# Eight layer norms on one core: the mean's scaling folded into its subtraction, and the squares moved to ScalarE in all but one of them

## The reference

```python
def _ln_c(v, eps=1e-06):
    m = jnp.mean(v, axis=-1, keepdims=True)
    s = jnp.var(v, axis=-1, keepdims=True)
    return (v - m) / jnp.sqrt(s + eps)
...
    x = x + _L0_conv_ref(_ln_c(x), ...)
    t = _to_tokens(x)
    t = t + _L0_ffn_ref(_ln_t(t), ...)
...
    x = x + _L3_conv_ref(_ln_c(x), ...)
    t = _to_tokens(x)
    t = t + _L3_ffn_ref(_ln_t(t), ...)
```

## Time and profile before

| what | value |
|---|---|
| median of three runs | 1205.78 us (1204.79 to 1205.86) |
| the profiled execution's own time | 1202.41 us |
| its span | 1200.6 us |
| PE busy | 747.2 us (62%) |
| PEld busy | 435.2 us (36%) |
| DVE busy | 479.7 us (40%), 828 instructions |
| ACT busy | 454.9 us (38%), 1547 instructions |
| POOL busy | 226.0 us (19%) |

### The profile page before, as it was taken

The page is one execution under the profiler, slowest core; times in us unless marked ns, Lnnn a source line. Parts: engine busy times, 40 slices in busy tenths (PEclk is TensorE's granted clock), DMA queues, the critical chain, the costliest instruction groups (busy, mean ns, idle before and its releaser), DMA issues. The chain is left out here.

```text
span 1200.6 us, 11335 instructions
## 1 busy us (share of the span) xinstructions
PE 747.2 (62%) x4114; PEld 435.2 (36%) x4114; DVE 479.7 (40%) x828; ACT 454.9 (38%) x1547; POOL 226.0 (19%) x130
## 2 busy tenths in 40 slices
PE   4807777777767655545555555557995555548975
PEld 1302222232233323223333333335773333325753
DVE  5597999999855534500000000012020000018652
ACT  3446556565424422033333333332212333335531
POOL 2276666666600000020000000000000000002200
PEclk9956999999995575555555555555555555555995
DMA  2020000000000000100000000000000000000000
GB/s 61 1 53 1 0 1 0 1 0 1 0 5 1 1 20 9 58 1 1 1 1 1 1 0 1 1 1 1 1 1 1 1 1 1 1 1 1 1 20 10
DMA packets 9570, 7.68 MB, mean 6 GB/s; under 512 B 7154, under 2 KB 8066, under 8 KB 9224
## 3 DMA queue, kind: packets, MB, share of 16 engines
q1 hardware_dynamic: 9512, 6.93, 2.4%
HBM read 5.09 MB, written 0.26 MB: 4 GB/s over the span
## 5 line engine op out<-in xcount | busy, mean ns | idle before, releaser
L791 PE MATMUL L2p_z<-L2yx,L2v 64*32 64x2 f32 x2048 | 267.9, 199 | 242.1 <-ACT L2yx L801 236.3
L801 ACT ACTIVATE L2yx<-L2p_z 32x2 f32<-32x2 f32 x1024 | 165.2, 161 | 389.2 <-PE L2p_z L791 389.2
L791 PEld LDWEIGHTS L2p_z<-L2yx,L2v 64*32 64x32 f32 x2048 | 180.4, 135 | 340.0 <-ACT L2yx L801 316.0
L692 DVE COPY xn<-L2yx 32x512 f32<-32x512 f32 x2 | 0.8, 417 | 431.1 <-ACT L2yx L801 264.2
L573 POOL TENSOR_TENSOR hc<-hs,cb 128x1024 f32<-128x1024 f32 x64 | 150.9, 2358 | 81.6 <-DVE hs L560 81.6
L560 DVE TENSOR_TENSOR_SCAN hs<-d_a,p_bb 128x1024 f32<-128x1024 f32 x64 | 146.3, 2286 | 8.9 <-ACT d_a L539 0.7
L526 PE MATMUL p_y<-hc,ident 128*128 128x512 f32 x256 | 122.5, 602 | 3.4 <-POOL hc L573 3.0
L1498 POOL COPY xo<-xn 64x256 f32<-64x256 f32 (+1 forms) x6 | 3.9, 691 | 555.9 <-DVE xn L157 555.9
L539 ACT ACTIVATE d_a<-step,decay 128x1016 f32<-128x1016 f32 x64 | 73.1, 1142 | 86.9 <-DVE hs L560 86.4
L510 PE MATMUL p_bb<-b_parts,pick 96*128 96x512 bf16 x128 | 40.5, 399 | 81.9 <-DVE hs L560 49.2
L555 DVE TENSOR_TENSOR p_bb<-drive,p_bb 128x1024 f32<-128x1024 f32 x64 | 77.3, 1207 | 6.2 <-PE p_bb L510 6.2
(11 more groups left out here) (387 smaller groups left out, 854.5 us busy)
## 6 DMA issues: line engine op xcount, KB each, us to landing
y_seq<-in_pick SPq DMA_DIRECT2D x1, 768.0 KB
b_parts<-part SPq DMA_DIRECT2D x3, 256.0 KB, 3.6
c_parts<-part SPq DMA_DIRECT2D x3, 256.0 KB, 4.4
pos<-in_pos SPq DMA_DIRECT2D x1, 512.0 KB, 3.6
ao<-in_at_o SPq DMA_DIRECT2D x1, 512.0 KB, 4.4
L1w<-in_L_w SPq DMA_DIRECT2D x1, 297.0 KB
L3w<-in_L_w SPq DMA_DIRECT2D x1, 297.0 KB
x_tok<-in_x SPq DMA_DIRECT2D x2, 128.0 KB, 2.8
```

What stands on the lines that cost most here:

```text
L791: pe.matmul(p_z[0:C, t % 2, 0:NB], v[:, 0:C], yx[:, NB * t:NB * (t + 1)], start=True, stop=True).then_inc(s("preact"), 1)
L801: act.activation(yx[0:C, NB * (t + 1):NB * (t + 2)], p_z[0:C, t % 2, 0:NB], ACT.Sigmoid).then_inc(s("state"), 1)
```

## The change

In every norm, the instruction that scales the sums (L139) goes, and the subtraction becomes one `scalar_tensor_tensor`, (sum x -1/32) + tile, with the constant in the instruction. In the seven norms whose halves alternate, ACT now makes the squares (function `Square`), after the load of the root's table and ahead of the roots, on a new semaphore `ln_centred`; DVE waits for it with `ln_squared`. In the norm with `apart=True` DVE still makes the squares. `ln_stat` has a row less. All else is as it was; the lines that follow in the file are two further down.

```diff
--- before.py
+++ after.py
@@ -83,7 +83,7 @@
         xn = sb("xn", [R, T])
         xn_tok = sb("xn_tok", [128, T // 128, R])
         ln_sq = sb("ln_sq", [128, 2, 4 * R])
-        ln_stat = sb("ln_stat", [128, 2, 5, 4 * NB])
+        ln_stat = sb("ln_stat", [128, 2, 4, 4 * NB])
         ln_warm = sb("ln_warm", [128, 1])
 
         ln_uses = [0]
@@ -106,7 +106,7 @@
 
             def step(self, i, h):
 
-                return sig["ln_step"], 10 * self.k + (5 * h + i if self.apart else 2 * i + h) + 1
+                return sig["ln_step"], 4 * self.k + (2 * h + i if self.apart else 2 * i + h) + 1
 
             def turn(self, pe, h, j):
                 t = (4 * h + j) * 128
@@ -136,21 +136,20 @@
                     dve.tensor_reduce(ln_stat[:, h, 0], by_token(self.turned[h]), AX_X, ALU.add).then_inc(sig["ln_step"], 1)
                 for h in hs:
                     dve.wait_ge(*self.step(0, h))
-                    dve.tensor_scalar(ln_stat[:, h, 1], ln_stat[:, h, 0], 1.0 / C, None, ALU.mult).then_inc(sig["ln_step"], 1)
+                    dve.scalar_tensor_tensor(by_token(tok(h)), spread(ln_stat[:, h, 0]), -1.0 / C, by_token(self.turned[h]),
+                                             ALU.mult, ALU.add).then_inc(sig["ln_centred"], 1)
+                if self.apart:
+                    for h in hs:
+                        dve.wait_ge(*self.at("ln_centred", h))
+                        dve.tensor_tensor(ln_sq[:, h], tok(h), tok(h), ALU.mult).then_inc(sig["ln_squared"], 1)
                 for h in hs:
-                    dve.wait_ge(*self.step(1, h))
-                    dve.tensor_tensor(by_token(tok(h)), by_token(self.turned[h]), spread(ln_stat[:, h, 1]), ALU.subtract).then_inc(sig["ln_step"], 1)
-                for h in hs:
-                    dve.wait_ge(*self.step(2, h))
-                    dve.tensor_tensor(ln_sq[:, h], tok(h), tok(h), ALU.mult).then_inc(sig["ln_step"], 1)
-                for h in hs:
-                    dve.wait_ge(*self.step(3, h))
-                    dve.tensor_reduce(ln_stat[:, h, 2], by_token(ln_sq[:, h]), AX_X, ALU.add).then_inc(sig["ln_square"], 1)
+                    dve.wait_ge(*self.at("ln_squared", h))
+                    dve.tensor_reduce(ln_stat[:, h, 1], by_token(ln_sq[:, h]), AX_X, ALU.add).then_inc(sig["ln_square"], 1)
                 for h in hs:
                     dve.wait_ge(*self.at("ln_sd", h))
-                    dve.reciprocal(ln_stat[:, h, 4], ln_stat[:, h, 3]).then_inc(sig["ln_step"], 1)
-                    dve.wait_ge(*self.step(4, h))
-                    dve.tensor_tensor(by_token(tok(h)), by_token(tok(h)), spread(ln_stat[:, h, 4]), ALU.mult).then_inc(sig["ln_scaled"], 1)
+                    dve.reciprocal(ln_stat[:, h, 3], ln_stat[:, h, 2]).then_inc(sig["ln_step"], 1)
+                    dve.wait_ge(*self.step(1, h))
+                    dve.tensor_tensor(by_token(tok(h)), by_token(tok(h)), spread(ln_stat[:, h, 3]), ALU.mult).then_inc(sig["ln_scaled"], 1)
                 if self.apart:
                     for h in hs:
                         dve.wait_ge(*self.at("ln_back", h))
@@ -158,11 +157,14 @@
 
             def act_roots(self, act, h):
                 act.wait_ge(*self.at("ln_square", h))
-                act.activation(ln_stat[:, h, 3], ln_stat[:, h, 2], ACT.Sqrt, bias=self.eps[:, 0:1], scale=1.0 / C).then_inc(sig["ln_sd"], 1)
+                act.activation(ln_stat[:, h, 2], ln_stat[:, h, 1], ACT.Sqrt, bias=self.eps[:, 0:1], scale=1.0 / C).then_inc(sig["ln_sd"], 1)
 
             def act(self, act):
 
                 act.activation(ln_warm[:], self.eps[:], ACT.Sqrt)
+                for h in range(2):
+                    act.wait_ge(*self.at("ln_centred", h))
+                    act.activation(ln_sq[:, h], xn_tok[:, 4 * h:4 * h + 4].rearrange("p j r -> p (j r)"), ACT.Square).then_inc(sig["ln_squared"], 1)
                 for h in range(2):
                     self.act_roots(act, h)
                 for h in range(2):
```

## The result

| | before | change |
|---|---|---|
| median, first runs | 1205.82 us (1204.79 to 1205.87, 4 runs) | 1197.13 us (1196.91 to 1198.47, 4 runs) |
| mean over more executions | 1204.3 us (74, all later) | 1197.4 us (9) |
| the profiled execution's own time, span | 1202.41, 1200.6 us | 1196.91, 1195.0 us |
| DVE, ACT, PE busy | 479.7, 454.9, 747.2 us | 473.9, 459.6, 747.5 us |

The ratio is 0.9932, 95% interval 0.9915 to 0.9949. The forecast was 1201.7 us with a range of 1199.9 to 1204.4: the direction was right, the gain was 8.7 us instead of 4.1, and the time fell outside the range. The second line already takes 1.8 us off the riddle: the four executions of the kernel before in the first line lay high, and over many the two kernels are 6.9 us apart. 6.9 is still not 4.1.

What follows compares the result with a forecast made beforehand. No engine is busy throughout, so time is a sum of stages, with DVE the one to relieve in the norms. Savings 3.15 + 0.63 + 0.13 + 0.20 = 4.11 us gave 1205.78 - 4.1 = 1201.7 us, range 1199.9 to 1204.4.

Steps and rivals of the forecast that it cites:

- The price of the folded form: Every norm: the one-instruction subtraction costs +0.00 us over the old one, +0.06 at most, saving the scaling's 0.20.
- ACT's square: Norms with alternating halves: a square of 256 elements on ACT takes 0.42 us, helping save 0.43 a norm.
- the handoffs: Norms with squares on ACT: passing from DVE to ACT takes 0.04 us and back 0.03.
- the 0.48 and 0.15 from under the memset: L0_ffn and L2_ffn: extra savings because the scaling held by POOL's memset is gone; 0.63 us together.
- the weights being late next in the expert blocks: Expert blocks: PE's gate load also waits for transfers, so 0.13 us of 1.26 is saved and 1.13 lost.
- the 0.20 in L3_conv: L3_conv norm: half 0 is hidden beside the recurrence; half 1 gains only the scaling, 0.20 us.
- Rival 1: Expert blocks: weights landed earlier than SP's wait tells, saving 1.26 us instead of 0.13; 5.2 saved, 1200.5; chance 0.08.
- Rival 2: L0_ffn, L2_ffn: POOL's memset holds the new subtraction as it held the scaling; 3.1 us saved, 1202.7; chance 0.12.
- Rival 3: Squares on ACT: square or handoffs take 0.43 us more, so handing over gains nothing; 1.96 left, 1203.8; chance 0.12.
- I take the same 4.1 off the median: Whole kernel: the 4.11 us summed from the profile comes off the median, 1205.78 - 4.1 = 1201.7.
- rival 4: L1_conv: PE's clock rises later, 0.4 us per pass, up to 8 us (1209.7); chance 0.10, of which 0.06 slower.

Runs made afterwards that it cites:

- Experiments 3: Kernel before with only the scaling folded into the subtraction in all eight norms, DVE still making the squares; 1200.97 us, ratio 0.9971.
- experiment 4: Kernel before with only the squares moved to ACT in seven norms, the scaling staying its own instruction; 1200.18 us, ratio 0.996.
- experiment 6: The change, with PE waiting only for the gate's two transfers before the logits and for the expert weights later; 1197.22 us, ratio 0.9945.
- experiment 5: Kernel before with POOL's memset in the two recurrent blocks moved behind the norm's last multiplication; 1203.74 us, ratio 0.9997.
- 7: Kernel before with four extra, overwritten 64-row matmuls ahead of the L1_conv convolution; 1205.29 us, ratio 1.0003.
- experiment 13: The change with two extra, overwritten matmuls filling PE's pause in the window attention; 1198.49 us, ratio 0.9954.
- 11: Kernel before with two overwritten 128-row matmuls filling PE's 2.0 us pause in the window attention; 1202.97 us, ratio 0.9989.
- 14: The change with both a delay of about 1.95 us after the second recurrence and PE's attention pause filled by two matmuls; 1200.43 us, ratio 0.9967.
- 10: The change with three waited-for DVE memsets behind the second recurrence, a delay of 1.95 us; 1201.52 us, ratio 0.9974.
- 12: The change with four overwritten 128-row matmuls ahead of the L1_conv convolution to warm PE's clock; 1197.98 us, ratio 0.9946.
- 15: The change with the gate's transfers waited for apart, 128-row warming matmuls before the convolution and PE's attention pause filled; 1196.96 us, ratio 0.9937.
- 8: The change with four extra, overwritten 64-row matmuls ahead of the L1_conv convolution; 1197.9 us, ratio 0.9947.

## Why the prediction was wrong in size

**The mechanism and each term held.** The price of the folded form (0.42, like a `tensor_tensor`), ACT's square (0.416), the handoffs (0.03 to 0.04), the 0.48 and 0.15 from under the memset, the weights being late next in the expert blocks, the 0.20 in L3_conv: the table of norms has them all, with 0.22 instead of 0.13 in the expert blocks. Experiments 3 and 4 separate the two halves of the change and find each at its price.

**Rival 1** (weights landed earlier) is refuted by the grown gap ending with the transfer, and by experiment 6. **Rival 2** (the memset holds the new subtraction) is refuted by the row at 354.73, and its premise, that the memset held the scaling, confirmed by experiment 5. By the rule that the prediction cited from the Trainium skill ("SBUF — State Buffer", section "SBUF: two separate sides"), the subtraction with one input in PSUM runs freely; the trace agrees (0.74 for two beside the memset, 0.74 elsewhere). The scaling pair's 0.66 beside the memset against 0.29 behind it is the measured other side. **Rival 3** (handing over is worth nothing) is refuted by experiment 4. The rule of the Trainium skill that wants multiplications on VectorE ("ScalarE: Activation LUTs", section "Rules for kernel authors") gives speed as its reason; here ACT's square was as quick (0.416 us), and the overlap of the halves was the gain.

**The step that failed** is the one between the sum and the time: "I take the same 4.1 off the median". It treated the norms' 4.1 us as the whole difference, and the clock as a matter of one to four passes in L1_conv, as likely to help as to hurt (rival 4). The clock's crossing in the L3_conv attention, which moves with everything ahead of it, was put at nothing without a look, and so was the pause behind it. Three things stood in the place of this step.

1. *The base.* The 1205.78 was the median of three high executions; 74 later ones average 1204.3. That is 1.5 us that have nothing to do with the change, and no row could have told it.
2. *The rise in the window attention.* Four profiles with the attention as in the kernel before (before twice, 5, 7) took 15.95 to 16.29 us for its start, 16.12 on average; the two profiles of the change took 15.28. That is 0.84 us. It rests on two executions: experiment 13, which is the change up to this point, took 15.94, and with it the difference is 0.62.
3. *The fall in the pause.* Three of these four had it and the two of the change had not: 0.9 us on average.

4.3 + 0.84 + 0.9 makes 6.0 of the 6.9 us between the means. The last 0.9 isn't placed, and the traces can hardly place it: the four profiled executions took 1203.5 us on average, 0.8 less than all 74, so most of it lies in executions that left no trace. The two halves of the change, each alone, fit the account: their profiles had the rise at 1.6 and 1.8 us, the attention's start at 15.43 and 15.47 and no fall, worth 0.7 and 0.9 us against the four, and they gained 1.1 and 1.6 us beyond their norms.

*Rival 4 in its own place.* The rise followed the block in the first two profiles: after three passes instead of four, 13.46 against 13.69 us for the L1_conv block. Over all profiles that have this block as it was and the norms of one of the two kernels, it took 13.61 to 14.51 us with the norms of before (five, mean 13.89) and 13.46 to 14.97 with those of the change (six, mean 13.91). So a later rise does cost single executions up to 1.5 us there, as rival 4 had it, and nothing on average. Early stages scatter as much: the one before the first scan took 3.06 us in one profile before and 2.90 in the other, 3.40 and 4.21 in the change, 2.8 to 4.3 in all.

**What the experiments show of the clock's part:** that the fall costs 1.2 us and happens in the pause (11, 14, and the table); that the delay of 10 costs 4.0 because it is 1.95 of delay, 0.7 to 1.1 of later rise (14 and 10 against the change) and 1.2 of fall; that the 1.4 us saved in the convolution were taken back by a later rise and the fall (12), and that with the pause filled the later rise remains (15).

**What they leave open:** why the profiles of one kernel mostly show nearly the same relation to the rise (2.8 and 3.0 us, 1.2 and 1.3 us), and where the last 0.6 to 0.9 us of the delay went in the kernel before. The two profiles of the change give a hint. Their sums of squares in the first norm stand 0.12 us apart (10.44 and 10.56 us), while the clock's changes stand 1.77 us later in the second (falls at 64.55 and 66.33). By 350 us the work too stands 1.75 us apart; the clock's rises in the attention are still 1.77 us apart (1098.79 and 1100.56), and the executions' own times differ by 1.67 us. So the second lost its time early and stayed in step with its clock from there on. That matmuls waiting for the clock do this is an argument, not a result. Experiment 13 shows that the step isn't fixed by the kernel: it is the change up to the attention, and its rise came at 2.8 us.

## What to carry to other kernels

A sum of traced pieces predicts the pieces; on a kernel that crosses PE's two clock levels several times, add to the range, on both sides, what each crossing *behind* the change can give or take: its passes at the lower level and every pause of PE that ends in slow matmuls. Look for such pauses in more than one profile of the kernel before, since its one profile here happened to lack the 1.2 us fall that the three other profiles with the same attention had. And test a small saving by its own stage as well as by the total: 0.6 us (5) and 1.1 us (6) were plain in their stages and not to be seen at the end.

## What was not expected of the hardware

- Four matmuls of 64 rows ahead of the convolution, in a stretch where PE was busy without a break, left the granted clock at 0.50 (8, and 7 in the kernel before); with 128 rows it rose at 423.6 us (12) and 424.7 (15), though PE was no busier. The row of the four 64-row matmuls:

```profile
419.49 7.08 PE L1050 MATMUL b1p_c<-x,ident 64*64 64x512 f32 x8
```

- Two DVE instructions of eight elements a partition took 0.66 us beside POOL's memset of a 32x2048 tile and 0.29 without it (5), while instructions of 256 elements with one input in PSUM ran at full speed beside it.
- A delay of 1.97 us on the path of every execution cost nothing that can be told in one kernel (mean -0.3 ± 0.4 us) and 4.0 us in one that differs in eight norms.
